# Expert weights in eight rotating buffers with their low halves, one scatter count per expert, no filler copies

## The reference

```python
scores = softmax(xf @ w_cls.T)                  # 64 choices: 32 experts, 32 zero experts
_, topk_idx = top_k(scores + bias, 8)
w = take(scores, topk_idx); w = w / (w.sum() + EPS) * 1.5
# expert e, on the rows routed to it (at most 256):
gu = buf @ w_gate_up[e]                         # 512 x 512
g, u = split(gu)
y = (silu(g) * u) @ w_down[e]                   # 256 x 512
routed_out = sum of w * y over the chosen experts
out = routed_out * (1 + sum of the zero experts' w)
```

## Time and profile before

| | us |
|---|---|
| median of 3 runs | 1022.58 (1015.96 to 1023.45) |
| the profiled execution | 1025.01 |
| its span, first to last instruction | 1023.2 |
| attention | about 0 to 510 |
| routing | about 510 to 740 |
| experts | 740.5 to 1023.2 |

### The profile page before, as it was taken

The page is one execution under the profiler, slowest core; times in us unless marked ns, Lnnn a source line. Parts: engine busy times, 40 slices in busy tenths (PEclk is TensorE's granted clock), DMA queues, the critical chain, the costliest instruction groups (busy, mean ns, idle before and its releaser), DMA issues. The chain is left out here.

```text
span 1023.2 us, 14443 instructions
## 1 busy us (share of the span) xinstructions
PE 905.2 (88%) x4313; PEld 731.7 (72%) x4313; DVE 771.3 (75%) x1837; ACT 503.7 (49%) x867; POOL 495.9 (48%) x420
## 2 busy tenths in 40 slices
PE   5789999999999999999699999999379897687960
PEld 3577888888888888888488888888357575566740
DVE  6978888888888888888777777776768767485720
ACT  5455555555555554555642333332258766475730
POOL 2456676666667666666400000000065566656652
PEclk9989999999999999999999999999679989797985
DMA  8001111111111111103755654431189979798743
GB/s 295 6 32 47 57 41 53 47 57 42 58 47 57 37 58 47 56 33 104 264 171 184 254 184 146 145 105 54 44 287 280 321 218 283 212 276 235 184 61 41
DMA packets 52758, 131.01 MB, mean 128 GB/s; under 512 B 12156, under 2 KB 14588, under 8 KB 46528
## 3 DMA queue, kind: packets, MB, share of 16 engines
q1 hardware_dynamic: 41248, 114.67, 32.4%
q0 software_dynamic: 11424, 15.29, 8.6%
HBM read 106.53 MB, written 35.91 MB: 139 GB/s over the span
## 5 line engine op out<-in xcount | busy, mean ns | idle before, releaser
L595 POOL TENSOR_TENSOR a_t<-a_t 128x512 f32<-128x512 f32 x80 | 105.2, 1315 | 101.7 <-DVE a_t L358 101.7
L1081 DVE TENSOR_TENSOR w_l<-raw,w_h 128x1024 fp32r<-128x1024 f32 x96 | 114.7, 1222 | 13.5 <-ACT w_h L1074 13.2
L604 POOL TENSOR_TENSOR a_fQ<-a_fQ,a_den 128x512 f32<-128x512 f32 x64 | 88.0, 1376 | 71.8 <-DVE a_den L396 71.8
L213 PE MATMUL a_PQ<-w_h,a_xT_h 128*128 128x512 f32 x384 | 107.8, 403 | 10.0 <-DVE w_l L345 9.3
L775 PE MATMUL r_PY<-w_h,r_o_h 128*128 128x512 f32 x256 | 106.3, 415 | 3.4 <-DVE r_o_l L867 3.4
L1179 POOL DMA_INDIRECT out<-m_y,si x38 | 66.2, 1741 | 88.0 <-DMA out<-m_y,si 64.5
L1051 POOL TENSOR_SCALAR r_vr<-r_mv 128x1 f32<-128x1 f32 x16 | 8.4, 526 | 199.0 <-DVE r_mv L878 199.0
L213 PE MATMUL a_PQ<-w_l,a_xT_h 128*128 128x512 f32 x384 | 104.2, 394 | 0.0
L213 PE MATMUL a_PQ<-w_h,a_xT_l 128*128 128x512 f32 x384 | 103.5, 392 | 0.0
L775 PE MATMUL r_PY<-w_l,r_o_h 128*128 128x512 f32 x256 | 101.9, 398 | 0.0
L775 PE MATMUL r_PY<-w_h,r_o_l 128*128 128x512 f32 x256 | 101.8, 398 | 0.0
(11 more groups left out here) (168 smaller groups left out, 2193.8 us busy)
## 6 DMA issues: line engine op xcount, KB each, us to landing
raw<-in_wgu SPq DMA_DIRECT2D x32, 1024.0 KB, 6.8
oT<-a_o SPq DMA_DIRECT2D x64, 256.0 KB, 2.5
raw<-in_wd SPq DMA_DIRECT2D x32, 512.0 KB, 6.4
v_l<-oT SPq DMA_DIRECT2D x11, 1024.0 KB, 6.6
v_h<-oT SPq DMA_DIRECT2D x5, 1024.0 KB, 6.7
out<-r_x SPq DMA_DIRECT2D x18, 256.0 KB, 2.0
a_xin<-in_x SPq DMA_DIRECT2D x16, 256.0 KB, 3.2
v_l<-in_wq SPq DMA_DIRECT2D x4, 1024.0 KB, 12.4
```

The costliest lines, as they stand in the source:

```text
L213: last = eng.matmul(bank[:, :], a[:, k, :], w[:, 4 * i + k, :], start=s == 0 and k == 0, stop=s == 2 and k == 3)
L595: eng.tensor_tensor(t1[:, r % 2, :], t1[:, r % 2, :], t2[:, r % 2, :], ALU.add).then_inc(sm["xr"], 1)
L604: eng.tensor_tensor(q, q, den[:, n % 2, :].unsqueeze(2).broadcast_to([P, 4, P]), ALU.mult).then_inc(sm["fs"], 1)
L1081: eng.tensor_tensor(low, src, high.bitcast(F32), ALU.subtract).then_inc(sm["m_wl"], 1)
```

## The change

Expert e uses entry e mod 8 of a ring. An entry has four parts: raw gate-and-up, raw down, and the low halves of both. Three entries are new memory, four lie over memory that `routing` used for the output projection (`v_l` for the raw weights, `w_l` for the low halves), and the eighth over ends of `v_h`, `w_h` and two new tiles. `w_h` keeps the high halves as before.

Loads: experts 0 to 2 as before; the gate-and-up part of expert 7 in chunk 5; experts 3 to 6 at the end of `routing`, when the last projection is done, on both sides of the last `store_w`; the down part of 7 at the start of `experts`. From expert 8 on, the gate-and-up load of e waits for PE's `up(e-8)` and the down load for PE's `down(e-8)`.

Scatters: one semaphore `m_s` gets 32 for each expert, 16 + 16 with two tiles and 32 from the only scatter with one. `no_scatter` with its filler copy and its wait is gone, and POOL's order for e is: gathers of e+6, flag, wait for e-1, scatter. The final wait for the scatters moves from POOL to SP.

Smaller things: the gather of a second tile no longer waits for the one before it in its buffer; in its first iteration PE does `up(0)` ahead of `turn(1)`; DVE clears all six second-tile row buffers first; ACT's first splits of weights no longer wait for the identity matrix.

```diff
-def routing(nc, sm, ..., gi, si, raw, wgu, wd, w_h_, w_l_, v_h, v_l):
+def routing(nc, sm, ..., gi, si, ring, wgu, wd, w_h_, w_l_, v_h, v_l):
...
                     if 2 <= c < 5:
-                        e = c - 2
-                        eng.dma_start(raw[e][:, 0:4, :], wgu[e]).then_inc(sm[f"m_wg{e}"], 16)
-                        eng.dma_start(raw[e][:, 4:6, :], wd[e]).then_inc(sm[f"m_wd{e}"], 16)
+                        load_up(sm, eng, ring, wgu, c - 2)
+                        load_down(sm, eng, ring, wd, c - 2)
+                    if c == 5:
+                        load_up(sm, eng, ring, wgu, 7)
                 for t in range(2):
                     eng.dma_start(out[T + t * P:T + (t + 1) * P, :], x2[:, 1, :]).then_inc(sm["r_so1"], 16)
+                eng.wait_ge(sm["r_y"], NC)
+                for e in (3, 4):
+                    load_up(sm, eng, ring, wgu, e)
+                    load_down(sm, eng, ring, wd, e)
                 store_w(NC - 1)
+                for e in (5, 6):
+                    load_up(sm, eng, ring, wgu, e)
+                    load_down(sm, eng, ring, wd, e)
...
+RING = 8
+
+def load_up(sm, eng, ring, wgu, e):
+    up, _, _, _ = ring[e % RING]
+    eng.dma_start(up, wgu[e]).then_inc(sm[f"m_wg{e % RING}"], 16)
...
+def parts(ring, w_h, e, part):
+    up, down, up_l, down_l = ring[e % RING]
     if part < 2:
+        i = 4 * (e % 3) + 2 * part
+        k = slice(2 * part, 2 * part + 2)
+        return pair(up[:, k, :]), pair(w_h[:, i:i + 2, :]), pair(up_l[:, k, :])
+    i = 12 + 2 * (e % 4)
+    return pair(down), pair(w_h[:, i:i + 2, :]), pair(down_l)
...
             @block.sync
                 eng.wait_ge(sm["m_g01"], 16)
-                for e in range(3, NE):
-                    eng.wait_ge(sm["m_wl"], 3 * (e - 3) + 2)
-                    eng.dma_start(raw[e % 3][:, 0:4, :], wgu[e]).then_inc(sm[f"m_wg{e % 3}"], 16)
-                    eng.wait_ge(sm["m_wl"], 3 * (e - 3) + 3)
-                    eng.dma_start(raw[e % 3][:, 4:6, :], wd[e]).then_inc(sm[f"m_wd{e % 3}"], 16)
+                load_down(sm, eng, ring, wd, 7)
+                for e in range(RING, NE):
+                    for t in range(2):
+                        eng.wait_ge(sm[f"m_gu{t}"], e - RING + 1)
+                    load_up(sm, eng, ring, wgu, e)
+                    for t in range(2):
+                        eng.wait_ge(sm[f"m_yd{t}"], e - RING + 1)
+                    load_down(sm, eng, ring, wd, e)
+                eng.wait_ge(sm["m_s"], 32 * NE)
...
             @block.gpsimd
-                        if t == 1:
-                            eng.wait_ge(sm[f"m_g1{e % 6}"], 16 * (e // 6))
...
-                def no_scatter(e):
-                    load_flag(eng, regs, e)
-                    with eng.If_lt(regs[e % 7], T):
-                        eng.wait_ge(sm["m_xt1"], e + 1)
-                    with eng.Else():
-                        eng.dma_start(spare[0:1, e % 2, :], consts[0:1, 0:16]).then_inc(sm[f"m_s1{e % 2}"], 16)
-
-                def scatter(e, t):
+                def scatter(e, t, done):
                     i = 2 * e + t
-                    if t == 0 and e >= 1:
-                        eng.wait_ge(sm["m_s0"], 16 * e)
-                        eng.wait_ge(sm[f"m_s1{(e - 1) % 2}"], 16 * ((e + 1) // 2))
...
                 for e in range(NE):
-                    no_scatter(e)
                     if e + 6 < NE:
                         gather(e + 6, 0)
                         gather(e + 6, 1)
-                    scatter(e, 0)
+                    load_flag(eng, regs, e)
+                    if e >= 1:
+                        eng.wait_ge(sm["m_s"], 32 * e)
                     with eng.If_lt(regs[e % 7], T):
-                        scatter(e, 1)
-                eng.wait_ge(sm["m_s0"], 16 * NE)
-                for i in range(2):
-                    eng.wait_ge(sm[f"m_s1{i}"], 16 * (NE // 2))
+                        scatter(e, 0, 16)
+                        scatter(e, 1, 16)
+                    with eng.Else():
+                        scatter(e, 0, 32)
...
             @block.tensor
                     both(eng, regs, e - 1, turn_a, "m_at1")
+                    if e == 0:
+                        both(eng, regs, 0, up, "m_gu1")
                     both(eng, regs, e + 1, turn, "m_xt1")
-                    both(eng, regs, e, up, "m_gu1")
+                    if e > 0:
+                        both(eng, regs, e, up, "m_gu1")
...
             @block.vector
-                clear(0)
-                clear(1)
+                for i in range(6):
+                    clear(i)
                 w_low(1, (0, 1))
                 load_flag(eng, regs, 0)
                 both(eng, regs, 0, x_low, "m_xTl1")
-                for i in range(2, 6):
-                    clear(i)
...
             @block.scalar
-                eng.wait_ge(sm["m_id"], 16)
...
                     if e >= 4:
-                        eng.wait_ge(sm["m_s0" if t == 0 else f"m_s1{e % 2}"], 16 * (e - 3 if t == 0 else e // 2 - 1))
+                        eng.wait_ge(sm["m_s"], 32 * (e - 3))
                     eng.activation(y[:, e % 4, t, :], PY[t][:, :], ACT.Copy).then_inc(sm[f"m_y{t}"], 1)
...
                 w_high(1, (0, 1))
+                eng.wait_ge(sm["m_id"], 16)
```

More of the change, by code:

```diff
@@ L628, in _, with routing @@
                         rstd(c + 1)
-def routing(nc, sm, x, wo, wc, bias, consts, oT, xn2d, out, gi, si, raw, wgu, wd, w_h_, w_l_, v_h, v_l):
+def routing(nc, sm, x, wo, wc, bias, consts, oT, xn2d, out, gi, si, ring, wgu, wd, w_h_, w_l_, v_h, v_l):
     with ExitStack() as ctx:
@@ L1101, in experts @@
         y = sb("y", [P, 4, 2, D])
-        spare = sb("spare", [1, 2, 16])
+        with nc.sbuf_tensor("m_raw", [P, 2, 512], F32) as raw:
+            pass
+        low = sb("low", [P, 2, 512], F32R)
         ident = sb("ident", [P, P])
@@ L1108, in experts @@
         PY = [ps("PY0"), ps("PY1")]
+        ring = ring + [(v_h[:, 20:24, :], raw[:, :, :], w_h[:, 20:24, :], low[:, :, :])]
         def f(ap):
@@ L1180, in scatter @@
                         out[:, :], bass.IndirectOffsetOnAxis(ap=si[:, i:i + 1], axis=0),
[L1181 removed]
+                        y[:, e % 4, t, :], None, compute_op=ALU.add).then_inc(sm["m_s"], done)
                 for e in range(6):
@@ L1372, in build @@
         si = ctx.enter_context(nc.sbuf_tensor("si", [P, 64], U32))
-        raw = [ctx.enter_context(nc.sbuf_tensor(f"raw{i}", [P, 6, 512], F32)) for i in range(3)]
-        routing(nc, sm, x, wo, wc, bias, cr, oT, xn2d, out, gi, si, raw, wgu, wd, w_h, w_l, v_h, v_l)
-        experts(nc, sm, wgu, wd, xn2d, out, gi, si, raw, cr, w_h, w_l)
+        with nc.sbuf_tensor("raw", [P, 18, 512], F32) as raw:
+            pass
+        low = ctx.enter_context(nc.sbuf_tensor("low", [P, 18, 512], F32R))
+        ring = [(v[:, i:i + 4, :], v[:, i + 4:i + 6, :], w[:, i:i + 4, :], w[:, i + 4:i + 6, :])
+                for v, w, n in ((raw, low, 3), (v_l, w_l, 4)) for i in range(0, 6 * n, 6)]
+        ring7 = ring + [(v_h[:, 20:24, :], None, None, None)]
+        routing(nc, sm, x, wo, wc, bias, cr, oT, xn2d, out, gi, si, ring7, wgu, wd, w_h, w_l, v_h, v_l)
+        experts(nc, sm, wgu, wd, xn2d, out, gi, si, ring, cr, w_h, w_l, v_h)
 def kernel(L0_attn_x, L0_attn_Wq, L0_attn_Wk, L0_attn_Wv, L0_attn_Wo, L0_ffn_w_cls, L0_ffn_bias,
```

50 lines of the change are left out of this document (25 added, 25 removed).

## The result

| | before | after |
|---|---|---|
| median of 20 runs each, us | 1019.51 (1006.72 to 1025.44) | 1028.18 (1018.96 to 1030.79) |
| the profiled execution, us | 1025.01 | 1020.98 |
| its span, us | 1023.2 | 1018.9 |

The ratio is 1.0095, 95% interval 1.0072 to 1.0118: the change makes the kernel slower by about 1%, where I forecast 2.3% faster.

What follows compares the result with a forecast made beforehand. POOL's serial scatters were taken to bound `experts`. Minus 5 (loads before 930), 3 (fillers), 12.1 (loads after) and 3.1 (end) made 23.2 us off the 1022.6 median: 999.4 us, range 984 to 1014.

Steps and rivals of the forecast that it cites:

- the chain that I had named as the bound: In `experts`, POOL's series of scatters, each waiting for a landing: 7.56 us a tile beside loads, 4.96 without.
- The 0.30 us that I did use from the earlier trace: Time POOL spends before any such instruction, counted as saved with each filler copy of 1.15 us.
- Loads after 930: From expert 19's scatter to the last, loads ending earlier leave eleven intervals load-free: 68.8 us against 80.9, minus 12.1.
- Loads before 930: Up to expert 19's scatter, loads moved into `routing` and falling about 2.7 us behind scatters: minus 5, range 0 to 10.2.
- Rival A: Loads get out of the scatters' way altogether and the stretch to 930 falls to its floor: 987 us; chance 0.17.
- Rival D: The 1.5 MB load pair goes out with the scatter, making intervals 9.1 instead of 7.56 us: 1030 us; chance 0.07.
- Rival C: With loads gone PE takes over as the bound at the end of `experts`: 1006 us; chance 0.12.
- Rival B: Loads are not the cause of long scatter intervals; mainly drain and fillers gain: 1010 to 1017 us; chance 0.14.
- Fillers and drain: In POOL's queue, dropped filler copies give minus 3; at the end, the drain starting before the last landing, minus 3.1.
- The start: First tile of `experts`: late gathers and gains such as `up(0)` ahead of `turn(1)` taken as equal: 0, range -2 to +5.
- The feared delay of the gathers by early loads: At the start of `experts`, loads of 5 and 6 in flight could make the first tile up to 4.1 us late.
- The base: The forecast took 23.2 us off the median of 1022.6, not off the profiled execution's 1025.0.
- Turns between queues: DMA engines alternating queues packet by packet would let a load add at most about 1.9 us to a scatter; not used in the sum.

Runs made afterwards that it cites:

- e1: The changed kernel with POOL's wait for the previous expert's scatters moved behind the branch, into both arms; ratio 0.9966 to the kernel before.
- e9: The kernel before with the new scatter part alone (one semaphore, no fillers, final wait on SP), but the wait inside both branch arms; ratio 0.9927.
- e3: The kernel before with the new scatter part alone (one semaphore, no fillers, final wait on SP), the wait ahead of the branch; ratio 1.0069.
- e5: The changed kernel with two repairs: the wait inside both branch arms, and turn(1) ahead of up(0) in PE's first iteration; ratio 0.9914.
- the second profile: The kernel before, unchanged, profiled once more; span 1015.5 us against 1023.2.
- e18: As e10, but SP reads a flag and branches four times before the loads, so they go out 2.3 us behind a scatter's start; ratio 0.9864.
- e10: As e5, but SP issues both loads of e on POOL's signal with the scatter of e-8, at -0.2 us from its start; ratio 1.0072.
- e19: As e18, but loads of e are tied to the scatter of e-11 and to PE's up and down of e-8; ratio 0.9867.
- e8: As e9, with the weight loads of experts 3 to 31 cut to 64 bytes a row; ratio 0.9517.
- e2: The changed kernel with PE's first iteration in its old order, turn(1) ahead of up(0); ratio 1.0014.
- e13: As e10, with POOL's signal placed behind the two gathers that follow the scatter; loads went out at +0.9 us; ratio 1.0296.
- e11: As e10, but SP first waits for an 8 KB copy of its own; loads went out mostly +5 to +8 us; ratio 1.0003.

## Why the prediction was wrong

**The step that was left out: the branch behind the wait.** I went through POOL's new order "gathers, flag, wait for e-1, scatter" and costed the filler and the gathers in it, but not that the branch, which had stood behind the first scatter, now stands between a landing and the next scatter. 0.66 us on each of 31 intervals is 20 us on the chain that I had named as the bound; 13 to 14 us of it show in the medians (e1 against after, e9 against e3). In the profiles the stretch from 19 to 31 shows about 7 us of it in each of these two pairs of kernels; the rest lies where loads run, where single profiles can't tell. With it the forecast of -23 would have been about -10. The 0.30 us that I did use from the earlier trace rows was the same kind of term.

**Loads after 930: right once the branch is out of the way.** 68.8 us forecast, 69.5 in e1 and 68.1 in e5. The gain of 12.1 that I took from it was too large, since the 80.9 us it is measured against were 77.3 in the second profile. After's 76.5 differs from the forecast by 7.7; twelve gaps of 0.66 are 7.9.

**Loads before 930: wrong, minus 5 to minus 8 forecast with the fillers, nothing found.** From 0 to 19 e5 takes 164.3 us, before 161.6 and 157.6. Two steps failed. The first is the sentence "PE's `down` is held until ACT's `y` copy of the expert before": it was the gather, and the pairs went out at scattered places. The second is what the place was to be worth. (88.55 - 5 - 5.4) / 11 = 7.1 us an interval at 2.7 us looks confirmed by e18's 7.02 at 2.3 us, but that is the mean of its one-tile intervals alone; its second tiles cost 13 us, where 7.1 + 2.7 = 9.8 was counted, and by the same sum its stretch gives (91.3 - 5.4) / 11 = 7.8 us, above the 7.56 that it was to improve. Rival A, with every pair at the good place and 78.3 us for this stretch, falls with it.

**Rival D.** Its mechanism is real, but its price was not: at its own place, with the scatter, a one-tile interval takes 8.3 us (e10), not 9.1; that +0.9 us gives 9.05 is a coincidence. In the changed kernel only part of the pairs fell there, and D's 1030 lies near the measured 1028 by luck, since the branch and the start made the difference. Rival C did not come: in the tail of e1 and e5, scatters follow each other every 5.0 us.

**Earliness is given back.** I added the tail's 12.1 us as if the stretch before did not know of it. e5 against e9 and e19 against e18 show the sum: loads that end earlier lie denser beside the earlier scatters. The tail gains 8 us (e5, e9) and the head loses 12 in those two profiles; the medians differ by less than 0.4%. Rival B comes nearest here, "the loads gain nothing", and e5's 1011.1 us lie in its 1010 to 1017, though not by its reason: the intervals without loads did fall to 5 us, and e8 shows that the loads cost 42 us.

**Fillers and drain: right in sum.** 6.1 forecast, 7 measured (e9, 3 us of uncertainty either way); the end is 9.2 us, though not by the parts that I had worked out.

**The start: right range, wrong sign.** I set the new order in PE's first iteration down as a gain. In its place the runs show a loss: 2 to 3 us at the first scatter, and 0.5% (e1 to e5) to 0.8% (after to e2) in the medians; what the rest of these 5 to 8 us is stays open. ACT's order was not read. The feared delay of the gathers by early loads did not come: the first three landed after 4.1 us (4.4 before), the next three after 4.6 (8.5 before).

**The base.** Taking the sum off a median was right, but the terms were read from one execution 5.5 us above the median. The stretch from 8 to 19 was no outlier (88.6 and 88.0 us); the one from 19 to 31, from which the largest term was taken, may have been (80.9 and 77.3).

Without the branch and the start the kernel takes 1011.1 us (e5), inside the range of 984 to 1014 and 12 us from the point; these two steps made it 1028. That it lies inside is partly the width of the range: e9 takes 1010.5 us without any of the new loads, from which 17 of the 23 us were to come.

**Turns between queues.** The records have 256 packets for a pair's two loads, 128 of them, 8 KB each, for the gate-and-up part; spread evenly over 16 DMA engines that is 8 packets, 64 KB, for each. In e10 the scatter's first packet came 4.8 us behind its start and the load's first at 0.8; 1 MB at the 351 GB/s of the window in which q1 held 97% takes 3.0 us. So the scatter's packets began about when the 1 MB load was through (0.8 + 3.0 = 3.8, its last packet at 4.2, and 4.8 measured), and ran beside the 0.5 MB one. I had argued that taking turns "packet by packet" would let a load cost a scatter 1.9 us at most, and found the intervals against it. That was a misreading. By the Trainium skill, "DMA: Bandwidth & Descriptors", section "Queues, rings and completion order", a DMA engine drains a whole packet from one ring before it switches, and a packet there is 9 to 17 descriptors as a rule and at most 64; I take what the records call a packet, one row of 8 KB, to be one descriptor's data. By that rule a turn can then be the engine's whole share of a load, and the trace agrees: 2.6 us without a packet of q0. It would also say why +2.3 us is cheap for the scatter beside it, which has its turn first. This is my reading and not shown: the records don't tell where a turn ends, and no run here varied the size of a load.

## What to carry to other kernels

List what an engine's sequencer executes between the event that releases the critical chain and the next link: here a branch behind the wait cost 0.66 us on every link, and the same branch ahead of it nothing that shows. (A flag read or a register move behind the wait would be the same kind of term; no run tried one.) Where a large transfer and a short serial one share the DMA engines, look where the large one's issue falls against the short one. Here +0.9 us was the dearest place, its start dear too, and 2.3 us behind it the cheapest, as long as no second short one follows within that time; against places that merely follow buffers the fixed one gained 0.5%, which isn't clear of the noise. Expect that transfers moved earlier take from the stretch they move into. Reorder one engine's queue only after reading the order of the engine it feeds.

## What the runs showed of the hardware that I had not expected

- An indirect DMA whose competitor (1.5 MB) is issued at -0.2, +0.9 and +2.3 us of its start repeats every 8.3, 9.05 and 7.0 us on average (one tile), against 5.0 us alone. Where two follow each other within 2 us, the same place (+2.4 us of the first) made it 13.0 and 13.2 us, against 9.7 at -0.2 us. A window of 2.6 us passed without one of its packets (e10).
- POOL's sequencer passes a semaphore signal while the DMAs that stand ahead of it in the program have not started (1.05 us ahead of the first gather in e13).
- POOL's drain at the block's end took 7.18 us when it began after the last landing, and 9.14 when it began with the last scatter (after). So starting it some 5 us earlier brought the end only 3 us nearer.
- An 8 KB copy, issued by SP, kept it waiting 1.6 to 9.2 us beside loads, 5.8 us in the median (e11).
